# The last key tile of an attention kernel: 65 keys put twice on 128 lanes, its value product in two matmuls, a ring of three probability tiles

## What is computed

```python
q = (query @ Wq + bq).reshape(B, L, NKV, G, HDIM)
k_, v_ = jnp.split(kv @ Wkv + bkv, 2, axis=-1)
...
scores = jnp.einsum('blkgd,bmkd->bkglm', q, k) * scale
attn = jax.nn.softmax(scores, axis=-1)
o = jnp.einsum('bkglm,bmkd->blkgd', attn, v).reshape(B, L, NHEAD * HDIM)
return o @ Wo + bo
```

## Time and profile before

| what | value |
|---|---|
| median of 3 runs | 2310.38 us (2306.56 to 2311.54) |
| the profiled execution | 2311.37 us |
| its span, first to last instruction | 2309.3 us |
| PE busy | 2262.2 us (98%), 12363 matmuls |
| DVE, ACT, POOL busy | 1815.1, 1666.7, 1633.0 us (79, 72, 71%) |
| mean granted clock of PE | 0.996 |
| DMA | 271.85 MB, mean 118 GB/s |

### The profile page before, as it was taken

How to read it: one execution, slowest core, us unless ns; L and a number is a source line. 1 busy time by engine, 2 the same in 40 slices (tenths; PEclk the granted TensorE clock), 3 DMA queues, 4 the chain that set the end, 5 groups by cost and what they waited for, 6 DMA issues and landing times.

```text
span 2309.3 us, 37402 instructions
## 1 busy us (share of the span) xinstructions
PE 2262.2 (98%) x12363; PEld 1941.8 (84%) x12363; DVE 1815.1 (79%) x3167; ACT 1666.7 (72%) x3152; POOL 1633.0 (71%) x1372
## 2 busy tenths in 40 slices
PE   7999999999999999999999999999999999999998
PEld 6888888887888888888888888888888888888865
DVE  5888888887887787787778787787787778787786
ACT  4777777776777777777777777777777777777772
POOL 4888786977568678757658678776767756766772
PEclk9999999999999999999999999999999999999999
DMA  7344353564233242326213333333422213222111
GB/s 258 121 167 133 111 173 100 173 199 162 87 111 111 94 160 94 133 79 209 92 43 137 116 128 116 111 127 118 157 86 96 92 60 110 66 98 90 66 68 55
DMA packets 137567, 271.85 MB, mean 118 GB/s; under 512 B 21664, under 2 KB 54944, under 8 KB 137120
## 3 DMA queue, kind: packets, MB, share of 16 engines
q1 hardware_dynamic: 122400, 255.71, 32.6%
q10 hardware_dynamic: 14976, 13.74, 2.6%
HBM read 202.44 MB, written 66.97 MB: 117 GB/s over the span
## 4 chain that ended last, share of the span: by engine, by line
PE 79%; DVE 9%; POOL 5%; issue 3%; ACT 3%; DMA 1%; ACTq 0%; SPq 0%; POOLq 0%; DVEq 0%
PE psW L432 12%; PE psW L434 11%; PE psW L433 11%; PE psS L432 7%; PE psS L434 7%; PE psS L433 7%; PE psW L656 6%; PE psW L657 6%; PE psW L658 6%; POOL xs L846 3%; PE psW L488 3%; DVE psum_ L1368 3%; DVE mrun L1335 2%; PE psW L496 1%; DVE pl L1105 1%
## 5 line engine op out<-in xcount | busy, mean ns | idle before, releaser
L846 POOL TENSOR_TENSOR xs<-xs,mb 128x512 f32<-128x512 f32 (+1 forms) x832 | 1068.9, 1310 | 472.3 <-ACT mb L917 472.3
L1335 DVE TENSOR_TENSOR mrun<-psS,mrun 128x512 f32<-128x512 f32 (+1 forms) x704 | 482.8, 686 | 340.1 <-ACT xs L917 337.5
L917 ACT ACTIVATE xs<-psS 128x512 f32<-128x512 f32 (+1 forms) x832 | 496.0, 596 | 245.1 <-PE psS L434 232.4
L1105 DVE TENSOR_TENSOR pl<-psP,ph 128x512 fp32r<-128x512 f32 (+1 forms) x672 | 459.8, 684 | 81.5 <-ACT ph L1047 76.2
L1047 ACT ACTIVATE ph<-xs 128x512 fp32r<-128x512 f32 (+1 forms) x832 | 518.9, 624 | 3.3 <-PE psW L658 3.1
L1368 DVE TENSOR_TENSOR psum_<-psP,psum_ 128x512 f32<-128x512 f32 (+1 forms) x672 | 457.4, 681 | 1.0 <-POOL pl L850 0.9
L1044 ACT ACTIVATE psP<-xs 128x512 f32<-128x512 f32 (+1 forms) x672 | 401.2, 597 | 29.4 <-DVE rinv L1268 12.9
L432 PE MATMUL psS<-ql,kh 128*128 128x512 f32 (+1 forms) x832 | 340.3, 409 | 6.3 <-DVE mrun L1335 5.2
L656 PE MATMUL psW<-ph,vh 128*128 128x512 f32 (+1 forms) x832 | 335.4, 403 | 3.6 <-POOL pl L850 3.3
L433 PE MATMUL psS<-qh,kh 128*128 128x512 f32 (+1 forms) x832 | 328.8, 395 | 0.0
L434 PE MATMUL psS<-qh,kl 128*128 128x512 f32 (+1 forms) x832 | 328.7, 395 | 0.0
(11 more groups left out here) (208 smaller groups left out, 4382.8 us busy)
## 6 DMA issues: line engine op xcount, KB each, us to landing
wqh<-scr_wq SPq DMA_DIRECT2D x96, 256.0 KB, 2.6
wql<-scr_wq SPq DMA_DIRECT2D x96, 256.0 KB, 3.0
woh<-scr_wo SPq DMA_DIRECT2D x48, 512.0 KB, 3.3
wol<-scr_wo SPq DMA_DIRECT2D x48, 512.0 KB, 4.2
rbc<-scr_r ACTq DMA_DIRECT2D x52, 256.0 KB, 3.4
scr_wq<-wqh SPq DMA_DIRECT2D x32, 256.0 KB, 2.1
scr_wq<-wql SPq DMA_DIRECT2D x32, 256.0 KB, 2.5
scr_wo<-woh SPq DMA_DIRECT2D x16, 512.0 KB, 2.6
```

The lines of the kernel that those rows point to most:

```text
L846: eng.tensor_tensor(tile, tile, mb[0:rows_of(t), U % 2, :], ALU.subtract).then_inc(s_sub)
L917: return eng.activation(hi, src, ACT.Copy)
L1105: return eng.tensor_tensor(lo, src, f32(hi), ALU.subtract)
L1335: eng.tensor_tensor(run, psS[0:rows, s % 2, :], a, ALU.max).then_inc(s_m)
```

## The change

Score tile 12 now has 128 lanes: keys 1536 to 1600 on lanes 0 to 64, and keys 1538 to 1600 again on lanes 65 to 127. ACT's exponentials then stand there twice too. The spare lanes of `vh` get the lower parts of those keys' values by a DMA, so that one matmul makes upper by upper and, for 63 keys, lower by upper. A second one has `vb` (upper values on lanes 0 to 64, the first two keys' lower values on lanes 96 and 97, zeros elsewhere) against `pl`, into whose lanes 96 and 97 DVE copies two rows of `ph`. The third matmul falls away. The rings `ph` and `pl` have three tiles.

```diff
-    RX, RP = 19, 4
+    RX, RP = 19, 3
+    LAST = LK - 128 * (NT - 1)
+    TWICE, SPARE = 2 * LAST - 128, 96
...
-                emptied(("k", K, c), s_kl, 4 * K + c + 1)
+                emptied(("k", K, c), s_kl, 5 * K + c + 1 + (c == 3))
...
+            def last_v(U, hs):
+                pe.wait_ge(s_vb2, 48 * (U // 4 + 1))
+                return vh[:, NT - 1, hs]
...
-                    eng.matmul(o, vh[0:rows, t, hs], hi, start=t == 0, stop=False)
-                    eng.matmul(o, vh[0:rows, t, hs], lo, start=False, stop=False)
-                    eng.matmul(o, vl[0:rows, t, hs], hi, start=False, stop=t == NT - 1).then_inc(s_pv)
+                    eng.matmul(o, vh[:, t, hs] if t < NT - 1 else last_v(U, hs), hi, start=t == 0, stop=False)
+                    if t < NT - 1:
+                        eng.matmul(o, vh[:, t, hs], lo, start=False, stop=False)
+                        eng.matmul(o, vl[:, t, hs], hi, start=False, stop=False).then_inc(s_pv)
+                    else:
+                        pe.wait_ge(s_l2, U + 1)
+                        n = SPARE + TWICE
+                        eng.matmul(o, vb[0:n, hs], pl[0:n, T % RP, :], start=False, stop=True).then_inc(s_pv)
...
+            def spread_v(P):
+                sp.wait_ge(s_vl, NT * (P + 1))
+                sp.wait_ge(s_vz, 1)
+                t = NT - 1
+                eng.dma_start(f32(vh[LAST:128, t, :]), f32(vl[TWICE:LAST, t, :])).then_inc(s_vb2, 16)
+                eng.dma_start(f32(vb[0:LAST, :]), f32(vh[0:LAST, t, :])).then_inc(s_vb2, 16)
+                eng.dma_start(f32(vb[SPARE:SPARE + TWICE, :]), f32(vl[0:TWICE, t, :])).then_inc(s_vb2, 16)
...
+                for kind, n, part in jobs.get(s - 2, []):
+                    if kind == "v" and part == NT - 1:
+                        spread_v(n)
...
-                if s == TN - 23:
+                if s == TN - 21:
...
+                if c == 3:
+                    eng.activation(kh[:, LK:128 * NT], bank_of(("k", K, c))[:, w - LAST + TWICE:w], ACT.Identity,
+                                   bias=bkv_sb[:, K % 8:K % 8 + 1]).then_inc(s_kh)
...
+                if c == 3:
+                    dve.wait_ge(s_kh, 5 * K + c + 2)
+                    eng.scalar_tensor_tensor(kl[:, LK:128 * NT], bank_of(("k", K, c))[:, w - LAST + TWICE:w],
+                                             bkv_sb[:, K % 8:K % 8 + 1], f32(kh[:, LK:128 * NT]),
+                                             ALU.add, ALU.subtract).then_inc(s_kl)
...
                     lower(pl[0:rows, T % RP, :], p, ph[0:rows, T % RP, :]).then_inc(s_l)
+                    if tt == NT - 1:
+                        eng.tensor_copy(pl[SPARE:SPARE + TWICE, T % RP, :], f32(ph[0:TWICE, T % RP, :])).then_inc(s_l2)
```

More of the change, by code:

```diff
@@ L183, in gated_block @@
         pl = sb("pl", [128, RP, 512], F32R)
-        kh = sb("kh", [128, LKP], F32R)
-        kl = sb("kl", [128, LKP], F32R)
+        kh = sb("kh", [128, 128 * NT], F32R)
+        kl = sb("kl", [128, 128 * NT], F32R)
         qh = sb("qh", [128, 2, 512], F32R)
@@ L219, in gated_block @@
         rtg = sb("rtg", [128, 4], F32)
+        vb = sb("vb", [128, 256], F32R)
         bvh = sb("bvh", [128, 1], F32R)
@@ L257, in gated_block @@
         s_rd = sem("s_rd")
+        s_vb2 = sem("s_vb2")
         s_s = sem("s_s")
@@ L293, in gated_block @@
         s_l = sem("s_l")
+        s_l2 = sem("s_l2")
+        s_vz = sem("s_vz")
         s_a = sem("s_a")
@@ L632, in _ @@
                     U, t = divmod(s, NT)
-                    rows = rows_of(t)
-                    ks = slice(128 * t, 128 * t + rows)
+                    ks = slice(128 * t, 128 * t + 128)
                     pe.wait_ge(s_ql, 2 * U + 2)
-                    pe.wait_ge(s_kl, 4 * (U // 2) + min(t // 3, 3) + 1)
+                    pe.wait_ge(s_kl, 5 * (U // 2) + min(t // 3, 3) + 1 + (t == NT - 1))
                     if s >= 2:
@@ L640, in _ @@
                             pe.wait_ge(s_m, 12 * ((s - 2) // NT) + (s - 2) % NT)
-                    three(psS[0:rows, s % 2, :], kh[:, ks], kl[:, ks], qh[:, U % 2, :], ql[:, U % 2, :]).then_inc(s_s)
+                    three(psS[:, s % 2, :], kh[:, ks], kl[:, ks], qh[:, U % 2, :], ql[:, U % 2, :]).then_inc(s_s)
                 T = s - VAL
@@ L654, in _ @@
                         pe.wait_ge(s_l, l_count[T])
-                    hi, lo = ph[0:rows, T % RP, :], pl[0:rows, T % RP, :]
-                    eng.matmul(o, vh[0:rows, t, hs], hi, start=t == 0, stop=False)
-                    eng.matmul(o, vh[0:rows, t, hs], lo, start=False, stop=False)
-                    eng.matmul(o, vl[0:rows, t, hs], hi, start=False, stop=t == NT - 1).then_inc(s_pv)
+                    hi, lo = ph[:, T % RP, :], pl[:, T % RP, :]
+                    eng.matmul(o, vh[:, t, hs] if t < NT - 1 else last_v(U, hs), hi, start=t == 0, stop=False)
[6 more added lines that the diff above has]
+                        eng.matmul(o, vb[0:n, hs], pl[0:n, T % RP, :], start=False, stop=True).then_inc(s_pv)
                 if s // NT >= 2 and s % NT == on_slot(s // NT - 2) + 2:
@@ L811, in _ @@
             eng.memset(ident[:, :], 0.0).then_inc(s_id)
+            eng.memset(f32(vb[:, :]), 0.0).then_inc(s_vz)
             pool.wait_ge(s_id, 1)
@@ L844, in take_off @@
                 pool.wait_ge(s_e, T + 1)
-                tile = xs[0:rows_of(t), T % RX, :]
-                eng.tensor_tensor(tile, tile, mb[0:rows_of(t), U % 2, :], ALU.subtract).then_inc(s_sub)
+                tile = xs[:, T % RX, :]
+                eng.tensor_tensor(tile, tile, mb[:, U % 2, :], ALU.subtract).then_inc(s_sub)
             def lower_p(T):
@@ L1012, in _ @@
                 if s < TN:
-                    t = s % NT
-                    rows = rows_of(t)
                     act.wait_ge(s_s, s + 1)
@@ L1017, in _ @@
                         act.wait_ge(s_h, s - RX + 1)
-                    upper(xs[0:rows, s % RX, :], psS[0:rows, s % 2, :]).then_inc(s_e)
+                    upper(xs[:, s % RX, :], psS[:, s % 2, :]).then_inc(s_e)
                 if sum_by_mem(V):
@@ L1046, in _ @@
                         act.wait_ge(s_pv, T - RP + 1)
-                    eng.activation(ph[0:rows, T % RP, :], xs[0:rows, T % RX, :], ACT.Exp).then_inc(s_h)
+                    eng.activation(ph[:, T % RP, :], xs[:, T % RX, :], ACT.Exp).then_inc(s_h)
                 for kind, n, part in jobs[s]:
```

4 lines of the change are left out of this document (3 added, 1 removed).

## The result

The changed kernel takes **2320.64 us** (median of 4 runs, 2320.22 to 2322.11) against 2308.47 us before (4 runs on the same chip, 2305.90 to 2311.54): a ratio of 1.0054, with a 95% interval of 1.0042 to 1.0066. So it is slower by 0.5%, inside the range and 6 us above the number that was predicted. The change itself is larger than forecast: +12.2 us between the medians, where the sum had +4.2; the base had been taken at 2310.4 us and came out 1.9 us lower. The profiled execution took 2320.22 us.

What follows compares the result with a forecast made beforehand. PE was taken to bound the kernel. The terms -14.9 (matmul) + 1.2 (end) + 1.6 (keys' copy) + 11.8 (small copies) + 4.5 (clock) = +4.2 us on 2310.4 gave 2314.6 us, range 2298 to 2323 us.

Steps and rivals of the forecast that it cites:

- What bounds the kernel: Whole kernel: PE, busy 2262.2 of 2309.3 us; a microsecond less there saves a microsecond unless a new wait opens.
- What is removed: 64 x 0.233 = 14.9 us: Last key tile of each unit: one value matmul less on PE, at its spacing of 0.233 us, 14.9 us less.
- (a) I take nothing: Slot 3 of each unit: DVE's copy of two rows into pl is hidden by 1.18 us idle time, cost nothing.
- The three small copies: Slot 5, units 14, 30, 46: PE waits for copies queued behind the context fetch, 3.9 us each, 11.8 us more.
- rival 1: Last tile's value matmuls: the small copies are not held up behind large transfers; 2298.3 us, chance 0.17.
- The clock behind each stall: Behind PE's three new stalls: granted clock falls, 1.5 us each, 4.5 us more, ends 0 and 9.
- rival 2: Units 14, 30 and 46: PE stalls, but the clock holds behind them; 2310.1 us, chance 0.13.
- The keys' second copy: Slot 7, units 14, 30, 46, 62: extra ACT and DVE operations lengthen PE's bank wait, 0.4 us each, 1.6 us more.
- The end and the ring: Last slots: with three tiles ACT waits for a later value product, delaying the final sum; 1.2 us more, ends 0 and 3.
- Rivals 3 and 4: 3: copies late behind value weights in nine units, 2323.6 us, chance 0.10; 4: gap between two matmuls, up to 2329, 0.03.

Runs made afterwards that it cites:

- drop third: The kernel before, with the third value matmul of the last key tile left out and nothing added: 2299.20 us, ratio 0.9959.
- a lighter POOL: The kernel before with a cheaper POOL operation for the weights' lower parts: 2300.08 us; the same without the last tile's third value matmul: 2289.33 us.
- copies first: The changed kernel with the three small copies issued a slot earlier, ahead of the context parts ch and cl: 2299.86 us, ratio 0.9963 to the kernel before.

## Why the prediction was right, and where it was not

**What bounds the kernel** and the spacing of 0.233 us are right: drop third gives 0.22 us on average in the units from 17 to 61.

**"What is removed: 64 x 0.233 = 14.9 us"** is the step that failed first: measured alone it is 9.4 us, and 10.8 with a lighter POOL. The sentence that a microsecond less of PE is a microsecond of time "unless a new wait opens" was then not applied to batch 0. There the matmul covered DVE's way to the sums' bank and to the running maximum, and its time came back as waits, in unit 4 with a slow clock behind one.

**"(a) I take nothing"** failed. The step looked for who waits behind the copy on DVE and found the running maximum, which has idle time. The instruction right behind it is the running sum, and POOL waits for that. It costs 0.4 us in each of eleven units, 4.4 us in all. The 0.69 us bound was about the right duration; the reader of the value was the wrong one.

**Nothing was said of the tensors' places.** With the longer key rows PE's 512-column matmuls follow each other faster: 4.1 us less in units 15 to 61, and a little more with the 128 lanes. In the 45 units this and the copy's 4.4 us cancel, so that they came to -0.22 us each. That is luck, and only looks like the forecast. The first error, in batch 0, is made up for by nothing.

**The three small copies**, the term that was to decide, did: the cause, the three units and no other, and the size, 4.10, 4.09 and 4.14 us for the 3.9 predicted and the ends of 3.4 and 4.6. The copies' issue took 0.65 to 0.86 us each on SP, which the sum took as 0; their landing had been set by what lies ahead of them anyway. One detail differs: in unit 14 `cl` landed at 517.07 + 7.6 = 524.7 and PE went on at 524.03, so the copies were done ahead of a transfer issued before them. This is the Trainium skill's rule that rival 1 rests on (DMA: Bandwidth & Descriptors, section Queues, rings and completion order): a later transfer may complete before an earlier one. The trace agrees with it in this unit; the copies were still held up by 4.1 us. **Rival 1 is wrong as stated**, and its number, 2298.3 us, is what one gets by issuing the copies first (2299.86).

**The clock behind each stall**: taken 1.5 us each, measured 1.86, 1.69 and 2.97, 6.5 in place of 4.5 us. That the clock falls is right and rival 2 is wrong. The term was sized by one slow stretch; behind unit 46 the low clock lasted through six microseconds.

**The keys' second copy** costs 0.22 us in each of four units and not 0.4: 0.9 for 1.6. **The end and the ring** cost 1.1 us from unit 62 on, with 0.2 of it the keys', for 1.2. Rivals 3 and 4 are wrong: no wait for the copies in the nine units, and none between the two matmuls.

Between traces the terms were +4.2 and came to +8.9. Of the 4.7 us between them units 1 to 13 have 3.3 (1.9 in unit 4), the three stalled units 1.8, the 45 units 0.7, and unit 62 with the end 0.4; the start and the first unit, where the clock was low for longer in the execution of before, give back 1.5. The rest of the way to 12.2 us is in the profiled executions: the one of before lay 2.9 us above the median of this comparison, the one after 0.4 below. What came, slower by more than 0.2%, had been given 0.40, and no change within 0.2% the most, 0.42.

## What to carry to other kernels

A small transfer that an engine is going to wait for belongs ahead of the bulk transfers in its queue; here one slot's difference was worth 18.9 us in three units and turned a slower kernel into a faster one. When an instruction is added to an engine with idle time, follow the reader of the very next instruction, on every engine, and not only the one that bounds: placed after the sum, the same copy cost nothing that shows. And before a removed instruction is priced at its full length in all stages, ask in each stage what it covered; with all of this the change is worth 0.65% (2293.01 us) where as written it costs 0.5%.

## What the runs showed of the hardware that was not expected

- A DVE copy from SBUF to SBUF beside POOL: 63 columns took from 0.18 to 7.98 us, a reduction of the same columns 0.20 to 0.21.
- Longer rows of two tensors, and not one instruction changed, shortened the start-to-start distance of 512-column matmuls by up to 4.5 ns (234.3 to 229.8), 4.1 us in units 15 to 61.
- The issue of a copy of 63 or 65 rows of 1 KB took SP 0.77 to 0.93 us (32 of them), that of a part of the context, `ch` or `cl`, 0.52 to 0.64 (24).
- The length of an idle time alone did not decide on the clock. At the same place in unit 4, PE idled 2.27 us in the changed kernel and 2.30 in the copies-first one, with the same work around it. Behind the first the granted clock was 0.50, behind the second 1.00, and in drop third it was 0.50 behind a shorter one, 1.96 us. What else decides is open. A fall in one execution and not in the other sets several of the traces above apart by 1.6 us in this unit. First the changed kernel, then copies first:

```profile
171.31 0.47 PE L669 MATMUL psW<-ph,vh 128*128 128x512 f32 x1 [2.27 <-POOL pl L882]
...
172.00:175.00 3.00, 3.00 (x15) 2.90 (x14) 1.90 (x5) 1.18 (x3) 3.00 (x4) 0.50 0.06 6
```

```profile
169.65 0.47 PE L669 MATMUL psW<-ph,vh 128*128 128x512 f32 x1 [2.30 <-POOL pl L882]
...
170.00:173.00 3.00, 3.00 (x21) 2.69 (x19) 1.90 (x5) 1.49 (x4) 3.00 (x3) 1.00 0.05 6
```
